# Indirect transfers without a gate and without a wait for their spacer, three buffers for gathered rows, and the last unit combined block by block

## The reference, cut to what matters

```
x = x + 0.5 * ffn(layernorm(x), gate_w, w1, w3, w2)
x = x + attn(layernorm(x), ...)          # shift-mix, k, v, r, wkv scan, output projection
x = x + 0.5 * ffn(layernorm(x), gate_w, w1, w3, w2)

def ffn(x, gate_w, w1, w3, w2):          # 8 experts, hidden size 512
    probs = softmax(x @ gate_w)
    expert_weights, expert_indices = top_k(probs, 2)
    expert_weights = expert_weights / expert_weights.sum(-1, keepdims=True)
    for i in range(8):
        wi = where(expert_indices == i, expert_weights, 0).sum(-1)
        out += (silu(x @ w1[i]) * (x @ w3[i])) @ w2[i] * wi
```

## Time and profile before

| what | value |
|---|---|
| median of 3 runs | 676.24 us (674.56 to 677.45) |
| the profiled execution's own time | 672.78 us |
| its span, first to last instruction | 671.0 us |
| mean granted TensorE clock | 0.946 |
| PE, PEld busy | 528.1 us (79%), 482.5 us (72%) |
| DVE, ACT, POOL busy | 412.7 us (62%), 319.7 us (48%), 297.2 us (44%) |

### The profile page before, as it was taken

One profiled execution on the slowest core, in us unless ns is written; L12 is line 12 of the kernel. 1 busy time (PEld: TensorE's weight loads), 2 busy tenths in 40 slices (PEclk: granted clock), 3 DMA queues, 4 the chain that ended last, 5 costly groups with the idle time before them and its releaser, 6 DMA issues. The chain is left out here.

```text
span 671.0 us, 18790 instructions
## 1 busy us (share of the span) xinstructions
PE 528.1 (79%) x5866; PEld 482.5 (72%) x5866; DVE 412.7 (62%) x1218; ACT 319.7 (48%) x703; POOL 297.2 (44%) x499
## 2 busy tenths in 40 slices
PE   2136899993899889898999859989789999989500
PEld 1125799893788878677888749878789899879500
DVE  4845975221678789588897848859786443333311
ACT  5433754441484566654656615854645344334100
POOL 1270356666540550565405655046005555525543
PEclk9999999998799999998999959999799999999955
DMA  8943234442221221222211133111112324322311
GB/s 287 325 143 99 84 112 147 136 134 67 76 77 41 64 72 49 73 64 63 78 49 45 53 99 83 44 60 49 57 34 77 100 81 127 85 64 72 86 52 43
DMA packets 89016, 59.57 MB, mean 89 GB/s; under 512 B 10208, under 2 KB 82656, under 8 KB 88928
## 3 DMA queue, kind: packets, MB, share of 16 engines
q1 hardware_dynamic: 55248, 29.97, 15.3%
q0 software_dynamic: 8192, 16.79, 8.9%
q10 hardware_dynamic: 25488, 11.61, 5.9%
HBM read 28.65 MB, written 29.69 MB: 87 GB/s over the span
## 5 line engine op out<-in xcount | busy, mean ns | idle before, releaser
L694 POOL DMA_INDIRECT rows_in<-parts,slot x128 | 132.5, 1035 | 232.9 <-DVE h L1084 136.4
L1084 DVE TENSOR_TENSOR h<-sil,pb 128x512 f32<-128x512 f32 x177 | 120.9, 686 | 145.8 <-PE pb L1201 59.3
L1215 PE MATMUL py<-ffn_w,h 128*128 x1416 | 199.0, 284 | 13.6 <-ACT yrow L753 12.4
L1215 PEld LDWEIGHTS py<-ffn_w,h 128*128 128x128 f32 x1416 | 175.3, 195 | 20.0 <-issue 13.9
L1201 PE MATMUL pa<-rT,ffn_w 128*128 128x128 f16 (+1 forms) x1752 | 152.7, 234 | 36.8 <-DVE h L1084 26.0
L708 POOL DMA_INDIRECT yg<-rows_out,slot x128 | 123.8, 968 | 130.3 <-issue 53.6
L1201 PEld LDWEIGHTS pa<-rT,ffn_w 128*128 x1752 | 124.9, 100 | 52.6 <-issue 41.1
L1201 PE MATMUL pb<-rT,ffn_w 128*128 128x128 f16 (+1 forms) x1752 | 157.1, 233 | 0.1
L1201 PEld LDWEIGHTS pb<-rT,ffn_w 128*128 x1752 | 124.4, 99 | 7.6 <-issue 0.3
L768 ACT ACTIVATE sil<-pa 128x512 f32<-128x512 f32 x177 | 105.4, 595 | 42.6 <-PE pa L1201 32.8
L748 ACT ACTIVATE rT<-pT 128x512 f16<-128x512 f16 (+1 forms) x112 | 56.8, 508 | 92.5 <-PE pT L1188 81.2
(11 more groups left out here) (155 smaller groups left out, 442.0 us busy)
## 6 DMA issues: line engine op xcount, KB each, us to landing
rows_out<-yrow ACTq DMA_DIRECT2D x177, 64.0 KB
rin<-rows_in SPq DMA_DIRECT2D x65, 128.0 KB
rows_in<-zrow SPq DMA_DIRECT2D x34, 128.0 KB
shared<-in_w SPq DMA_DIRECT2D x16, 256.0 KB, 7.0
rin<-rows_in SPq DMA_DIRECT2D x47, 64.0 KB
rows_in<-zrow SPq DMA_DIRECT2D x2, 1472.0 KB, 12.2
xres<-in_x SPq DMA_DIRECT2D x4, 512.0 KB, 5.7
ffn_w<-in_w SPq DMA_DIRECT2D x8, 256.0 KB
```

Source lines behind the costliest of these rows:

```text
L694: pool.indirect_dma_start(rows_in[g][:], bass.IndirectOffsetOnAxis(ap=slot[:, c, at:at + 1], axis=0), parts[:, at, :], None).then_inc(s_sc ...
L1084: dve.tensor_tensor(h[:, t % RING, :], sil[:, t % 2, :], pb[t % 2][:], ALU.mult).then_inc(s_h, 1)
L1215: mm = pe.matmul(py[:], h[:, step % RING, at:at + T], w, start=(c == 0), stop=(c == FC - 1))
```

## The change

Six things change.

1. An indirect transfer no longer waits for a tile (`s_h`) nor for the memset ahead of it. The memset stays between two transfers, grows from 64 to 192 elements a partition, and writes one of four parts of `pace`; it waits only for the memset four places back.
2. `yg` gets three buffers, used in turn by the order of the gathers (`GSLOTS`), where it had one for each unit of a run.
3. In the last unit each block has its own semaphore (`s_last`), `combine_last` combines block by block, both choices of a block after each other, and SP writes each block by itself.
4. The planner's clock gets other numbers: an up product of unpaired tiles of 0.73, others of 0.66, landing of 4.5, a spacing of 1.55, and other slips. So steps move by a tile or so.
5. The planner holds a gather back by the three buffers instead of the two.
6. The final wait counts the added writes.

```diff
--- before.py
+++ after.py
@@ -75,11 +75,13 @@
 XSLOTS = 3
 SLOTS = 6
 YSLOTS = 10
+GSLOTS = 3
 RING = 6
 SKEW = 3
 FILLED_FIRST = 2
 FILL = 256
-PACE = 64
+PACE = 192
+PACES = 4
 
 
 NORM = ("stats", "rsqrt", "norm", "hi", "lo", "turn", "xnT", "logits", "keep")
@@ -110,10 +112,10 @@
         "pe": {"turn": 0.45, "logits": 0.9, "turn_m": 0.85, "pk": 1.3, "pv": 1.3, "pr": 1.3, "count": 0.9, "out": 0.9},
         "sp": {"write": 0.0, "scatter": 0.0}}
 ENGINE = {step: eng for eng in WORK for step in WORK[eng]}
-UP, TURN, DOWN, COPY_T, COPY_Y, SILU, H = 0.67, 0.055, 0.92, 0.3, 0.28, 0.6, 0.69
-HOP, LAND, SEND, LOAD = 0.1, 4.0, 1.1, 3.0
-SLIP = {"dve": 6.0, "act": 3.1, "pe": 2.0}
-SPACE = 1.6
+UP, UP_ALONE, TURN, DOWN, COPY_T, COPY_Y, SILU, H = 0.66, 0.73, 0.055, 0.9, 0.3, 0.28, 0.6, 0.69
+HOP, LAND, SEND, LOAD = 0.1, 4.5, 1.1, 3.0
+SLIP = {"dve": 6.5, "act": 3.1, "pe": 1.4}
+SPACE = 1.55
 
 
 EARLY = -1
@@ -185,11 +187,12 @@
     def tile(self, t):
 
         q, half, _ = TILE_OF[t]
-        up1 = max(self.free["pe"], self.rT[q] + HOP, self.h.get(t - 2, 0.0) + HOP) + UP
+        up = UP if paired(t) else UP_ALONE
+        up1 = max(self.free["pe"], self.rT[q] + HOP, self.h.get(t - 2, 0.0) + HOP) + up
         if t > SKEW:
             self.free["act"] = self.y[t - SKEW - 1] = max(self.free["act"], self.down + HOP) + COPY_Y
         turned = self.turn(q + 1, up1) if t + 1 < TILES and TILE_OF[t + 1][1] == 0 else up1
-        up3 = turned + UP
+        up3 = turned + up
         silu = max(self.free["act"], up1 + HOP) + SILU
         self.h[t] = self.free["dve"] = max(self.free["dve"], silu + HOP, up3 + HOP) + H
         self.free["act"], self.free["pe"] = silu, up3
@@ -310,12 +313,16 @@
 
         waiting.append([due, at, name, run, [(b, j, c) for b in units for j in range(JU) for c in range(TOPK)]])
 
+    def in_use(run, unit):
+
+        order = [p[2:] for p in plan if p[1] == "gather"]
+        n = order.index((run, unit))
+        return n >= GSLOTS and "combine" not in gathered[order[n - GSLOTS]].ends
+
     def send(tile, until):
 
         while True:
-            now = [w for w in waiting if w[1] <= until and not (w[2] == "gather" and any(
-                c.next() == "combine" for c in chains if c.unit == w[4][0][0] and gathered.get((c.run, c.unit)) is c
-                and c.run < w[3]))]
+            now = [w for w in waiting if w[1] <= until and not (w[2] == "gather" and in_use(w[3], w[4][0][0]))]
             at = max([free["pool"]] + [min((w[1] for w in now), default=until)])
             if not now or at >= until:
                 return
@@ -385,6 +392,9 @@
     return order.index(upto) + 1
 
 
+GATHERS = [p[2:] for p in PLAN if p[1] == "gather"]
+
+
 def run_of(t):
 
     return max(r for r in range(RUNS) if START[r] <= t)
@@ -443,7 +453,7 @@
         upper = sb("upper", [P, P], BF16)
         ones16 = sb("ones16", [P, P], BF16)
         zrow = sb("zrow", [P, 2 * D], F16)
-        pace = sb("pace", [P, PACE], U8)
+        pace = sb("pace", [P, PACES, PACE], U8)
         e_desc = sb("e_desc", [P, JG, E])
         t_iota = sb("t_iota", [P, max(PASS_STEPS)])
 
@@ -488,7 +498,7 @@
         sil = sb("sil", [P, 2, FC * T])
         h = sb("h", [P, RING, FC * T])
         yrow = sb("yrow", [P, YSLOTS, D])
-        yg = sb("yg", [P, UG, TOPK, JU, D])
+        yg = sb("yg", [P, GSLOTS, TOPK, JU, D])
         qkv_f = yg[:].rearrange("p b c j d -> p (b c j) d")[:, 0:6, :]
 
         xT = sb("xT", [P, 2, 2, S + 2], F16)
@@ -556,7 +566,9 @@
         s_y = sem("down_done")
         s_yrow = sem("y_copied")
         s_yst = [sem(f"y_stored{i}") for i in range(YSLOTS)]
-        s_gat = [sem(f"gathered{b}") for b in range(UG)]
+        s_gat = [sem(f"gathered{i}") for i in range(GSLOTS)]
+        s_last = [sem(f"last_gathered{j}") for j in range(JU)]
+        s_lastc = sem("last_combined")
         s_comb = sem("combined")
         s_min = sem("minmax_made")
         s_exp = sem("exps_made")
@@ -647,6 +659,11 @@
             def step(name, run, b):
                 if name == "write":
                     u, js = units(run, b)
+                    if (run, b) == GATHERS[-1]:
+                        for j in range(JU):
+                            sp.wait_ge(s_lastc, j + 1)
+                            sp.dma_start(ov[:, js, :][:, j, :], xres[:, js, :][:, j, :]).then_inc(s_out, 16)
+                        return
                     sp.wait_ge(s_comb, count(("combine",), ("combine", run, b)))
                     sp.dma_start(ov[:, js, :], xres[:, js, :]).then_inc(s_out, 16)
 
@@ -663,7 +680,7 @@
                 for _, name, run, b in (p for p in PLAN if p[0] == t < TILES):
                     step(name, run, b)
             last_steps(step)
-            sp.wait_ge(s_out, 16 * B)
+            sp.wait_ge(s_out, 16 * (B - 1 + JU))
 
 
         @block.gpsimd
@@ -700,28 +717,26 @@
                 if (b, j, c) == (0, 0, 0):
                     for k in range(YSLOTS):
                         pool.wait_ge(s_yst[k], 16 * len(range(k, PEND[run], YSLOTS)))
-                if (j, c) == (0, 0):
-                    before = [p[1:] for p in PLAN if p[1] == "gather" and p[3] == b]
-                    at_b = before.index(("gather", run, b))
-                    if at_b:
-                        pool.wait_ge(s_comb, count(("combine",), ("combine", before[at_b - 1][1], b)))
+                n = GATHERS.index((run, b))
+                if (j, c) == (0, 0) and n >= GSLOTS:
+                    pool.wait_ge(s_comb, count(("combine",), ("combine", *GATHERS[n - GSLOTS])))
                 pool.indirect_dma_start(
-                    yg[:, b, c, j, :], None, rows_out[SET[run]][0:PASS_STEPS[PASS[run]] * T, :],
-                    bass.IndirectOffsetOnAxis(ap=slot[:, c, at:at + 1], axis=0)).then_inc(s_gat[b], 16)
+                    yg[:, n % GSLOTS, c, j, :], None, rows_out[SET[run]][0:PASS_STEPS[PASS[run]] * T, :],
+                    bass.IndirectOffsetOnAxis(ap=slot[:, c, at:at + 1], axis=0)).then_inc(
+                        s_last[j] if n + 1 == len(GATHERS) else s_gat[n % GSLOTS], 16)
 
             def every(run, units):
                 return [(run, b, j, c) for b in units for j in range(JU) for c in range(TOPK)]
 
             for one in every(0, range(UNITS[0])):
                 scatter(*one)
-            for sent, (gate, name, *one) in enumerate(TRANSFERS):
-                wait(pool, s_h, gate)
-                wait(pool, s_pace, sent)
+            for sent, (_, name, *one) in enumerate(TRANSFERS):
                 if name == "scatter":
                     scatter(*one)
                 else:
                     gather(*one)
-                pool.memset(pace[:], 0).then_inc(s_pace, 1)
+                wait(pool, s_pace, sent - PACES + 1)
+                pool.memset(pace[:, sent % PACES, :], 0).then_inc(s_pace, 1)
             for run in range(RUNS):
                 for one in every(run, range(UNITS[run] if PEND[run] == TILES else 0)):
                     gather(*one)
@@ -1086,17 +1101,31 @@
             def combine(run, b):
 
                 u, js = units(run, b)
-                runs = [p[2] for p in PLAN if p[1] == "gather" and p[3] == b]
-                dve.wait_ge(s_gat[b], 16 * TOPK * JU * (runs.index(run) + 1))
+                n = GATHERS.index((run, b))
+                dve.wait_ge(s_gat[n % GSLOTS], 16 * TOPK * JU * (n // GSLOTS + 1))
                 for c in range(TOPK):
                     for j in range(JU):
                         xj = xres[:, js, :][:, j, :]
-                        ins = dve.scalar_tensor_tensor(xj, yg[:, b, c, j, :], wts[:, c, u * JU + j:u * JU + j + 1],
-                                                       xj, ALU.mult, ALU.add)
+                        ins = dve.scalar_tensor_tensor(xj, yg[:, n % GSLOTS, c, j, :],
+                                                       wts[:, c, u * JU + j:u * JU + j + 1], xj, ALU.mult, ALU.add)
                     if c == 0:
                         link(ins)
                 ins.then_inc(s_comb, 1)
                 dve.wait_ge(s_comb, count(("combine",), ("combine", run, b)))
+
+            def combine_last(run, b):
+
+                u, js = units(run, b)
+                slot_ = (len(GATHERS) - 1) % GSLOTS
+                for j in range(JU):
+                    xj = xres[:, js, :][:, j, :]
+                    dve.wait_ge(s_last[j], 16 * TOPK)
+                    for c in range(TOPK):
+                        ins = dve.scalar_tensor_tensor(xj, yg[:, slot_, c, j, :],
+                                                       wts[:, c, u * JU + j:u * JU + j + 1], xj, ALU.mult, ALU.add)
+                        if c == 0:
+                            link(ins)
+                    ins.then_inc(s_lastc, 1)
 
             def step(name, run, b):
                 u, _ = units(run, b)
@@ -1104,7 +1133,7 @@
                 if name == "split":
                     split(b)
                 if name == "combine":
-                    combine(run, b)
```

(1 more changed line is left out.)

## The result

The changed kernel took **819.66 us** (818.13 to 825.22, 4 runs) where the kernel before took 676.85 (674.56 to 677.63, 4 runs): ratio **1.2132**, 95% interval 1.2063 to 1.22. The forecast of 637.5 was wrong, and so was its sign. Repeated later on two chips, the same unedited program took 822.5 on the one and **621.7** on the other, where its ratio was **0.9218** (0.9188 to 0.9247). The kernel before took 675.6 and 675.7 beside them. So the result has two halves: what the change does to the kernel's own waits, and something that is there on some chips and not on others.

A forecast was written before the change was run, and what follows sets the result against it. POOL's sending pace was taken to bound the kernel. Savings of 11 + 5 + 5 + 17.7 = 38.7 us from the profiled 672.8 gave 634.1, or 637.5 against the median of 676.2; range 626 to 660.

The forecast's parts named there:

- So what matters is how fast POOL sends: Whole kernel: POOL bounds the end and mid-kernel stalls wait for gathered rows, so POOL's sending pace counts.
- The first stall: At 152 to 170 us, DVE waits for gathered rows; wait gone up to spacing 1.61, 11 us (7 to 15.6).
- The cost of a transfer afterwards: Spacing of POOL's transfers: 0.95 transfer, 0.24 memset, 0.30 idle, so 1.50 us (bounds 1.25 and 1.95).
- The second stall: At 384 to 392 us, PE waits at tile 101 for run 5's scatters; wait gone, 5 us (2 to 6).
- The small waits: Ten waits, 18.0 us together; data some 3 us earlier, worth 5 us (2 to 9).
- The tail: From tile 161's store to the end: earlier, closer gathers, third buffer, shorter last combine and write; 17.7 us saved.
- What costs nothing: Early writes, the memset's wait four transfers back and other planner numbers: zero, with 3 us to each side.
- Slower: Rival, 6 in 100: transfers take the long form; spacing 2.2 gives 697 us, 2.5 gives 727.
- The rule of the Trainium skill: GpSimd and DVE lock a shared port pair; GpSimd-issued DMAs wait out some DVE operations, at worst every transfer long.

The follow-up runs named there:

- e12: The changed kernel, not edited, on a chip without late PE updates: 621.7 us, ratio 0.9218 to the kernel before.
- Run 0: Not a follow-up run: a group of the kernel's own work, whose sixteen transfers lie at 27 to 50 us; no time of its own measured.
- e3: The kernel before with only the gate (wait for the tile's h) taken from the transfers, memset wait kept: spacing 1.41 us, 155 late PE updates.
- C: A chip without late PE updates; the changed kernel with memsets of 320, 432 and 560 elements, 64 at the end, took 622.8, 625.5 and 634.5 us.
- E: A chip without late PE updates; the unedited changed kernel took 621.7 us there.
- e7: The kernel before with only the three buffers and the block-wise end of the change: 0.9% below the kernel before.
- D: A chip with late PE updates; the unedited changed kernel took 822.5 us there.
- fast end: Edit of the changed kernel: memset of 64 elements behind the last eight spaced transfers; with 432 elements elsewhere, 625.5 or 655.7 us by chip.
- B: A chip with late PE updates; the changed kernel with a memset of 432 elements throughout took 644.6 us there.
- F: A chip with late PE updates; the changed kernel with 432 elements, and 64 behind the last eight spaced transfers, took 655.7 us there.
- e8: The changed kernel with a memset of 432 elements, and 64 behind the last eight spaced transfers: 625.5 us.
- run 5: Not a follow-up run: a group of the kernel's own work, at tile 101, which needs its 16 scatters; no time of its own measured.

## Why the prediction was wrong, step by step

The changed kernel on the better chip (e12): its page, its stretch of 125 to 170, and DVE and POOL at the first combine and at the end. They answer to the earlier trace rows.

```profile
span 618.6 us, 18561 instructions
...
PE 517.2 (84%) x5866; PEld 475.1 (77%) x5866; DVE 415.2 (67%) x1218; ACT 317.9 (51%) x703; POOL 324.5 (52%) x499
...
PE   1234799899999999998999959999989999989940
...
PE 57%; ACT 13%; DVE 10%; issue 9%; POOL 6%; DMA 2%; POOLq 0%; ACTq 0%; DVEq 0%
```

```profile
125.00:170.00 45.00, 44.75 (x477) 41.98 (x476) 23.14 (x69) 23.83 (x56) 39.17 (x63) 1.00 0.46 127
```

```profile
151.98 1.17 DVE L1109 SCALAR_TENSOR_TENSOR xres<-yg,wts,xres 128x128 f32<-128x128 f32 x4
...
608.21 0.94 POOL L723 DMA_INDIRECT yg<-rows_out,slot  x1 [0.30 <-issue]
608.95 2.89 SPq L665 DMA_DIRECT2D out<-xres  x2
610.74 0.74 DVE L1124 SCALAR_TENSOR_TENSOR xres<-yg,wts,xres 128x128 f32<-128x128 f32 x2 [1.82 <-DMA yg<-rows_out,slot]
```

- **The step that failed: "So what matters is how fast POOL sends", with every term priced as if PE, ACT and DVE kept their pace at any spacing.** In "The first stall" the tiles were to reach DVE's combine at 152.3; in the result they are slowed by the transfers meant to serve them. The first combine came at 209.78 instead of 165.39, and the last store at 797.41 instead of 631.96. The trace of before had a sign of it that I had not looked for: 90 of its 605 updates of PE are 0.05 to 0.8 us late, all for work that ended 0.4 to 1.4 us behind a transfer's start, while no other engine's is over 0.02. How large it would grow could not be read there: behind 60 us it sends no two transfers under 1.84 apart but the eight of run 8, when PE is done. Run 0's sixteen, at 27 to 50 us, are mostly 1.27 apart, but only 4 updates of PE fall there, in time.
- **"The cost of a transfer afterwards", 1.50:** 1.40. The memset took 0.27, not 0.24; the idle time 0.17, not 0.30. My reading that 0.45 belonged to the waits was right in size (e3: 0.47), but it was the doubling of the waits, the gate's on top of the memset's.
- **"The first stall", 11:** right in mechanism where the updates are in time. The combine at 151.98 has no wait ahead of it, PE is busy 44.75 of 45 us, and tile 35's `h` begins at 154.4 instead of 169.1: 14.7, so nearly all of the 15.6 came home. The bound of 1.61 for the spacing held too: on C 1.51 and 1.60 give 622.8 and 625.5, and 1.71 gives 634.5, where the first combine waits 3.8 us again.
- **"The second stall", 5, and "The small waits", 5:** none of DVE's ten waits for gathered rows between 171 and 632, 18.0 us, is left on E (one of 6.9 us, for run 7's rows, stands in the tail), and PE's 4.08 at tile 101 is gone. The tiles gained 13 more up to tile 101 and 7 more up to 161, so 20 instead of 10. Mis-sized: I had charged most of it off against stretches with PE at 92%.
- **"The tail", 17.7:** from tile 161's store to the end it was 73.05 and is 55.65 on E: **17.4**. Within it the write of a block was mis-sized: from the last combine's end to the program's end it takes 7.1 us where it took 5.4, in e7 as well, so minus 1.8 and not plus 0.75; the shorter spacing made that up. In the result run 8's tiles lie beside run 7's gathers, and the tail took 82.6.
- **"What costs nothing":** the planner's numbers were not tested apart.
- **"Slower", 6 in 100:** the right sign by the wrong mechanism. It needed long transfers, and the median stayed at 0.967. The rule of the Trainium skill, page "SBUF — State Buffer", section "SBUF: two separate sides", which I had set against the change, is about DVE and POOL holding up each other; the runs hardly show it growing, as 14 of the 256 transfers took over 1.2 us before, 18 on E and 11 in the result, and no rule there is about PE's updates.

In sum: on E the terms were 35 and 17.4 instead of 21 and 17.7, which is 52 us of the span and 54 of the median (675.7 to 621.7), just below the range; on D, and in the result, a cost of some 200 us stood against them that no term held. The version to keep is 432 elements: it beat the kernel before on all chips that had it (0.928 to 0.930 on C and E with the fast end, 0.952 on B without it, 0.971 on F with it). The fast end is better left out: it cost some 10 us on F, and what C and E would lose without it was not measured (2.5 us by e8's forecast). The changed kernel is the fastest of all where it is fast (621.7) and the slowest where it is not.

## What to carry to other kernels

A pause between transfers that looks like waste may be what keeps another engine's signals in time: before taking it out, sweep its length, and look in the changed trace not only at the engine that was sped up but at when its neighbours see each other's results. And look for small signs in the trace of before: one engine's updates at up to 0.8 us, where all others are at 0.01, was the sign here. Where a consumer starts long after its producer's end and its releaser is no instruction, compare the time of the semaphore update itself with the end of the work. And run a change that raises a rate on more than one chip before believing its time: the kernel before was within 0.5% on all, this one was 621.7 or 822.5.

## What was not expected of the hardware

- On four of six chips (and in the result) PE's semaphore updates come over 1 us late, by up to 16.6 us, while POOL makes indirect transfers 1.60 us or less apart in the kernel; at 1.87 they come 0.9 us late at most. Those of DVE, ACT and POOL do not (0.04 us at most). On two chips none of PE's is over 0.03 us late, down to 1.40 in the kernel and, on C, 1.25 in the bench. Spacings of 1.40, 1.51, 1.60 and 1.71 cost 621.7, 622.8, 625.5 and 634.5 there. On the others 1.40, 1.51 and 1.87 cost 822.5, 722.8 and 663.8, and 1.60 cost 644.6, or 655.7 with the fast end.
- Plain transfers from POOL or SP and memsets on POOL don't bring it; 32 rows do as much as 128, and rows of 128 bytes as much as those of 512. Beside groups of a single product it did not show.
- POOL's idle time ahead of an indirect transfer was 0.17 us with no wait, 0.28 with one for the memset just ahead, 0.16 with one for a gate met long ago, and 0.75 with both.
- A write of the last unit in four parts ends 7.1 us behind the last combine, in one part 5.4.
